# Unpacking 4-bit weights of the last layer during an earlier attention instead of during the attention just before it

## The chip, the core and the metric

The kernel runs on one core of a Trainium2 chip. A core has a matrix engine (TensorE, PE in the rows; PEld is its weight load), three engines for elementwise work (VectorE = DVE, ScalarE = ACT, GpSimd = POOL) and SyncE (SP), which here only issues DMA transfers. Each engine works through its own list of instructions in order; the lists are tied together by semaphores alone. The metric is the device time of one execution in microseconds (us).

## What is computed

The state x has 8 batches of 128 rows by 512 (float32). Four layers run over it; each is an attention over `ctx_4096` and a feed-forward part, both added to x:

```python
x = x + _L2_xattn_ref(_layernorm(x), ctx_4096, mask, Wq, Wk, Wv, Wo, ...)   # wide attention: 32 heads of 128
x = x + _L2_ffn_ref(_layernorm(x), weight)                                   # product of values rounded to fp8
x = x + _L3_xattn_ref(_layernorm(x), ctx_4096, ctx_4096)                     # lag attention: FFT, top lags, softmax
x = x + _L3_ffn_ref(_layernorm(x), w1, s1, w2, s2, w3, s3)                   # silu(x W1) * (x W3), then W2
```

W1, W3 (1376 x 512) and W2 (512 x 1376) come packed. Each 32-bit word holds one byte with two signed 4-bit values, `w >> 4` and the sign-extended low four bits; each group of 64 values has one float32 scale:

```python
msb = w >> 4
lsb = (w & 15 ^ 8) - 8
deq = concatenate([msb, lsb], 1).reshape(-1, 64) * s[:, None]
```

## The kernel before

The layers before L2 are not touched. From there on four stages follow each other, each ended by `end_stage`, a barrier that all engines meet: `wide_attention`, `quantised_ffn`, `lag_attention`, `streamed_packed_ffn`.

**wide_attention** runs over steps s: 8 groups of 4 heads times 8 batches are 64 steps, with some ten steps of weight preparation ahead of step 0 and five behind step 63. In a step PE makes the scores of batch s, the queries of s + 4, a quarter of the next group's keys or values, the mix of s - 3 and the output projection of s - 4; each engine has its fixed list of such parts. Matmuls are done in three passes on float16 halves (`pair_matmul`, lines 67 to 69). DVE's list of a step begins with `low_of_heads` (tile a_o_lo), `maxima` (a_masked, a_negmax: the softmax's mask and maximum, which wait for the step's scores) and `add_to_x` (x_state); `add_to_x` frees the one bank into which PE puts the next output projection. SP turns queries, keys and probabilities by DMA (DMA_TRANSPOSE) and loads the next group's weights.

**quantised_ffn** loads, on SP, the tables of the lag attention (`spectra.load`), and then all packed words that the next two stages need first: W2's words and scales (`load_down`), and the first 128 rows of W1 and W3 (`load_first`, "the first tile"). SP waits for them at the stage's end.

**lag_attention** takes batches through a pipeline of steps i = 0 to 10 (`over_steps`): DVE multiplies the query spectra by the key spectra (tile x_q_prod), PE turns them into correlations, DVE finds the nine largest of each row (MAX8 and MATCH_REPLACE8 on x_nine, x_left), PE and DVE form the output. `AHEAD` splits the layer norm that opens the stage into batches 0, 1 and the rest. W2 is prepared here by `DownWeight` in 11 chunks of 512 values:

- `unpack` (DVE): two tensor_scalar shifts of 128x256 int32 into `ints`;
- `to_half` (ACT): to float16, over the place of the words; `UNPACK` says when: chunks 0 to 2 and 3 to 6 ahead of the first step, 7 and 8 in step 0, 9 and 10 in step 1;
- `scale` (POOL): times the scales; `high` (ACT) and `low` (POOL): split into two float16 halves; SP turns a quarter of W2 whenever its chunks are ready.

At the stage's end the layer norm of the last part begins: ACT normalises batches 0 to 3 (`rows_ahead`), DVE takes their low halves (`low_of_row`), SP turns them (`turn_row`). Between these stand the same five operations for the first tiles of W1 and W3; SP's last two issues of the stage, `turn_first`, wait for POOL's `low` of them.

**streamed_packed_ffn** begins with PE's product of batches 0 to 3 and the first tile of W1 (`first_in`, `xt_in` are what it waits for). The other tiles of W1 and W3 are unpacked while it runs.

Of the kernel before, what the change touches and what calls it, by code (L numbers as in the profile page):

```python
# [8 lines left out]
P = 128  # L9
B = 8  # L10
DIM = 512
KT = DIM // P
EPS = 1e-5
WS = 64.0
# [1376 lines left out]
def wide_attention(K, A, wq, wk, wv, wo, mask=None, qw=None, kw=None, quant=None, nxt=None):  # L1391
# [12 lines left out]
    with ExitStack() as c:  # L1404
# [131 lines left out]
        with nc.Block() as block:  # L1536
            @block.sync
            def _(sp):
# [22 lines left out]
                for s in steps:  # L1561
# [149 lines left out]
            def _(act):  # L1711
# [68 lines left out]
                for s in steps:  # L1780
# [10 lines left out]
                    for u in live(s):  # L1791
                        exponentials(u)

            @block.vector
            def _(dve):
# [92 lines left out]
                for s in steps:  # L1888
# [30 lines left out]
            def _(pool):  # L1919
# [723 lines left out]
def quantised_ffn(K, Q, spectra, packed):  # L2643
# [8 lines left out]
    with ExitStack() as c:  # L2652
# [7 lines left out]
        largest_done, chain, words_here = (K.sem(f"f2_{n}") for n in ("largest", "chain", "words"))  # L2660
# [193 lines left out]
def lag_attention(K, S, packed):  # L2854
# [9 lines left out]
    with ExitStack() as c:  # L2864
# [18 lines left out]
        UNPACK = {-2: (0, 1, 2), -1: (3, 4, 5, 6), 0: (7, 8), 1: (9, 10)}  # L2883
        ROWS = packed.FIRST_ROWS
        W1, W3 = down.FIRST["w1"], down.FIRST["w3"]
# [19 lines left out]
        with nc.Block() as block:  # L2905
            @block.sync
            def _(sp):
                packed.load_scales(sp)
                for i in range(B + 2):
# [76 lines left out]
            def _(act):  # L2986
# [64 lines left out]
                for i in (-2, -1):  # L3051
                    for chunk in UNPACK[i]:
                        down.to_half(act, chunk)
# [3 lines left out]
            def _(dve):  # L3057
# [10 lines left out]
                def step(f, m, l, n, j, i):  # L3068
# [6 lines left out]
                    for chunk in UNPACK.get(i, ()):  # L3075
                        down.unpack(dve, chunk)
# [759 lines left out]
```

## Time and profile before

| | |
|---|---|
| median of 3 runs | 1548.2 us (1547.27 to 1550.75) |
| the profiled execution's own time | 1544.96 us |
| its span, first to last instruction | 1543.2 us |
| mean granted clock of TensorE | 0.964 of full speed |
| busy: PE, DVE, ACT, POOL | 90%, 69%, 49%, 46% of the span |

The span is what the trace shows in detail; 1.8 us of the profiled execution lie around it. Its time is 3.2 us below the median of the runs, so sums made in the trace are carried to the median as differences.

### The profile page before, as it was taken

What the parts mean: (1) busy time and instruction counts of PE and PEld (TensorE: products, weight loads), DVE (VectorE), ACT (ScalarE), POOL (GpSimd) and SP (SyncE); (2) the same over time, 40 slices, a digit from 0 to 9 for tenths busy, and PEclk for the clock granted to TensorE, in tenths of its full rate; (3) what the DMA queues carried; (4) which work ended last, traced back from release to release, by engine and by line L of the source; (5) the groups of instructions that cost most, each with busy time, mean ns of one, the idle gap of its engine ahead of it and who ended that gap; (6) DMA issues with size and microseconds to landing.
All of it is one profiled execution on the core that took longest, in us unless ns stands there. A gap on an engine that the chain in (4) does not pass through costs nothing. (4 is left out here: it accounts for less than half of the span.)

```text
span 1543.2 us, 31400 instructions
## 1 busy us (share of the span) xinstructions
PE 1385.5 (90%) x11336; PEld 829.9 (54%) x11352; DVE 1068.9 (69%) x2142; ACT 752.6 (49%) x2417; POOL 717.0 (46%) x736
## 2 busy tenths in 40 slices
PE   5898599997999999659999999999998677879998
PEld 4776244445777777326555555555554234434444
DVE  7997565636667766558878878788778789956212
ACT  4677363223434433237666666666654356555111
POOL 4887451002434435726666666666555115744000
PEclk9999799999999999989999999999999789989999
DMA  7999572216999988556666566544434402456000
GB/s 184 187 172 175 128 167 39 41 28 147 176 183 188 164 147 144 96 133 153 122 132 114 117 129 122 107 112 108 103 73 83 145 3 41 102 89 111 16 18 28
DMA packets 524138, 174.63 MB, mean 113 GB/s; under 512 B 482528, under 2 KB 507424, under 8 KB 523856
## 3 DMA queue, kind: packets, MB, share of 16 engines
q1 hardware_dynamic: 523984, 172.62, 57.9%
q8 instruction: 92, 1.51, 0.4%
q14 instruction: 62, 0.51, 0.1%
HBM read 53.27 MB, written 2.10 MB: 36 GB/s over the span
## 5 line engine op out<-in xcount | busy, mean ns | idle before, releaser
L1929 POOL TENSOR_TENSOR a_q_ss<-a_q_ss,half 128x4 f32<-128x4 f32 x64 | 89.3, 1395 | 183.5 <-DVE a_k_ss L1845 93.0
L67 PE MATMUL bank<-a_wq_hi,xn_pair 128*128 128x512 f16 (+1 forms) x384 | 139.8, 364 | 20.3 <-DVE a_wq_lo L1880 16.9
L1764 ACT ACTIVATE a_probs<-a_masked,a_negmax 128x128 f32<-128x128 f32 x256 | 99.6, 390 | 95.6 <-DVE a_negmax L1816 95.6
L1286 POOL TENSOR_TENSOR a_p_hl<-a_probs,a_p_hl 128x512 f16<-128x512 f32 x64 | 74.3, 1161 | 142.5 <-DVE a_p_hl L1210 142.5
L68 PE MATMUL bank<-a_wq_lo,xn_pair 128*128 128x512 f16 (+1 forms) x384 | 139.7, 364 | 0.0
L69 PE MATMUL bank<-a_wq_hi,xn_pair 128*128 128x512 f16 (+1 forms) x384 | 139.6, 364 | 0.0
L67 PE MATMUL bank<-a_wo_hi,a_o_hi 128*128 128x512 f16 x256 | 98.0, 383 | 9.9 <-DVE x_state L1832 9.9
L69 PE MATMUL bank<-a_wo_hi,a_o_lo 128*128 128x512 f16 x256 | 98.0, 383 | 0.0
L68 PE MATMUL bank<-a_wo_lo,a_o_hi 128*128 128x512 f16 x256 | 98.0, 383 | 0.0
L1813 DVE TENSOR_TENSOR a_masked<-bank,a_mask 128x512 f32<-128x512 f32 x64 | 44.1, 690 | 70.2 <-PE bank L69 70.1
L1944 POOL TENSOR_TENSOR a_normal<-a_probs,a_recip 128x512 f32<-128x512 f32 x64 | 89.7, 1401 | 5.0
L716 POOL TENSOR_TENSOR a_p_hl<-a_probs,a_p_hl 128x512 f16<-128x512 f32 x64 | 78.3, 1234 | 25.4 <-DVE a_p_hl L627 15.1
L67 PE MATMUL bank<-a_k_t,a_q_t 128*128 128x128 f16 (+1 forms) x384 | 81.1, 237 | 0.4 <-DMA a_q_t<-a_q_hl 0.4
L69 PE MATMUL bank<-a_k_t,a_q_t 128*128 128x128 f16 (+1 forms) x384 | 81.0, 237 | 0.0
L68 PE MATMUL bank<-a_k_t,a_q_t 128*128 128x128 f16 (+1 forms) x384 | 81.0, 237 | 0.0
L489 ACT ACTIVATE a_probs<-bank,a_negmax 128x128 f32<-128x128 f32 x256 | 72.3, 380 | 17.6 <-DVE a_negmax L620 17.3
L1775 ACT ACTIVATE a_o_hi<-bank 128x512 f16<-128x512 f32 x64 | 38.1, 596 | 86.3 <-PE bank L69 86.2
L1203 DVE TENSOR_REDUCE a_negmax<-bank 128x2 f32<-128x512 f32 x64 | 42.8, 690 | 50.3 <-PE bank L69 50.3
L3666 DVE SCALAR_TENSOR_TENSOR f_h<-bank,f_h 128x512 f32<-128x512 f32 (+1 forms) x22 | 15.2, 689 | 85.6 <-PE bank L69 76.0
L1130 ACT ACTIVATE a_probs<-bank,a_negmax 128x256 f32<-128x256 f32 x128 | 53.3, 472 | 32.5 <-DVE a_negmax L1203 32.5
L1732 ACT ACTIVATE a_qn<-bank 128x128 f32<-128x128 f32 x256 | 67.1, 288 | 3.1 <-PE bank L69 3.1
L1937 POOL TENSOR_TENSOR a_recip<-a_total,minus_one 128x4 f32<-128x4 f32 x64 | 64.8, 1012 | 6.9 <-ACT a_probs L1764 6.9
(459 smaller groups left out, 4983.0 us busy)
## 6 DMA issues: line engine op xcount, KB each, us to landing
a_no<-in_L_xattn_Wo SPq DMA_DIRECT2D x9, 1024.0 KB, 5.9
a_nq<-in_L_xattn_Wq SPq DMA_DIRECT2D x8, 1024.0 KB, 5.8
a_n_wq<-in_L_xattn_Wq SPq DMA_DIRECT2D x4, 768.0 KB, 5.8
a_n_wo<-in_L_xattn_Wo SPq DMA_DIRECT2D x4, 768.0 KB, 5.4
a_nk<-in_L_xattn_Wk SPq DMA_DIRECT2D x9, 256.0 KB, 3.0
a_nv<-in_L_xattn_Wv SPq DMA_DIRECT2D x9, 256.0 KB, 4.0
f_v_hat<-in_L_ffn_w SPq DMA_DIRECT2D x2, 1152.0 KB, 5.9
x_state<-in_x SPq DMA_DIRECT2D x8, 256.0 KB, 4.2
```

Source lines behind the costliest of these rows:

```text
L67: pe.matmul(out, lh, rh, start=start, stop=False)
L68: pe.matmul(out, lh, rl, start=False, stop=False)
L69: return pe.matmul(out, ll, rh, start=False, stop=stop)
L489: m = act.activation(probs[t % PS][:, h * P:(h + 1) * P], s_bank[t][:, h * P:(h + 1) * P], ACT.Exp, bias=negmax[t % 4][:, h:h + 1])
L716: pool.tensor_tensor(p_hl[t % PS][:, 1, :], probs[t % PS][:, :], p_hl[t % PS][:, 0, :], ALU.subtract).then_inc(plo_done.sem, 1)
L1130: m = act.activation(probs[u % PROBS][:, n, :], s_bank[(s, t)][:, n * KTL * P:(n + 1) * KTL * P], ACT.Exp, bias=negmax[u % 4][:, n:n + 1])
L1286: pool.tensor_tensor(p_hl[s % PN][:, 1, t, :], probs[unit(s, t) % PROBS][:, :, :].rearrange("p h n -> p (h n)"), p_hl[s % PN][:, 0, t, :], ...
L1732: m = act.activation(dst[:, h, :], src[:, h, :], ACT.Square, scale=1.0 / WS, accum_out=sums[:, h:h + 1])
L1764: m = act.activation(probs[s % 2][:, h, :], src, ACT.Exp, bias=negmax[s % 2][:, h:h + 1], accum_out=total[s % 2][:, h:h + 1])
L1929: pool.tensor_tensor(r[:, :], r[:, :], K.half[:, 0:n], ALU.pow).then_inc(root_done.sem, 1)
L1937: pool.tensor_tensor(recip[s % 2][:, :], total[s % 2][:, :], K.minus_one[:, :], ALU.pow).then_inc(recip_done.sem, 1)
L1944: m = pool.tensor_tensor(normal[s % 2][:, t, :, :], probs[s % 2][:, :, t * P:(t + 1) * P], by, ALU.mult)
```

## The change

`PackedFirst` is new. It holds the packed words, their scales and the first tiles in memory of its own from the wide attention on, loads them there, and does three things in the wide attention's steps: `unpack` on DVE, `halves` on ACT and `scale_first` on POOL, each called as the last or nearly last part of its engine's step. Thirteen pieces (first tile of W1, of W3, then W2's 11 chunks) take their turn every fourth step from step 3 on. Piece n has its two shifts on DVE at steps 3 + 4n and 5 + 4n and its copy to float16 on ACT at 6 + 4n; the two first tiles are also scaled on POOL at 8 + 4n, split on ACT at 9 + 4n and on DVE at 10 + 4n. The rows of `xn_rows`, unused until the wide attention's end, serve as `ints` and `flat`. In the lag attention `unpack` and `to_half` are gone, `scale`, `high` and `low` of W2's chunks stay, and nothing of the first tiles is left but `turn_first`, which SP now issues in step 7.

```diff
@@ wide_attention: SP, ACT, DVE, POOL, at the end of a step
+                    down.load(sp, s)
...
+                    down.halves(act, s)
...
+                    down.unpack(dve, s)
                     if 0 <= s - ROWS - 1 < quant.ahead:
                         row_ahead(s - ROWS - 1)
...
+                    down.scale_first(pool, s)
@@ quantised_ffn, SP
                 spectra.load(sp)
-                packed.load_down(sp, words_here)
-                packed.load_first(sp, words_here)
-                sp.wait_ge(words_here, 96)
@@ lag_attention, SP
+                    if i == B - 1:
+                        sp.wait_ge(qb_bank.filled("x"), qb_bank.n_filled("x", B - 1))
+                        for m in ("w1", "w3"):
+                            packed.turn_first(sp, m)
...
-                for m in ("w1", "w3"):
-                    sp.wait_ge(down.lo_done.sem, down.lo_done.count(down.FIRST[m]))
-                    packed.turn_first(sp, m)
@@ lag_attention, ACT and DVE (in a step, at the stage's end, and ahead of the steps)
-                    for chunk in UNPACK.get(i, ()):
-                        down.to_half(act, chunk)
...
                         rows_ahead(0)
-                        down.to_half(act, W1)
                         rows_ahead(2)
-                        down.to_half(act, W3)
-                        down.high(act, W1)
-                        down.high(act, W3)
...
-                for chunk in UNPACK[-1]:
-                    down.unpack(dve, chunk)
                 over_steps(step)
@@ lag_attention, POOL
                 over_steps(step)
-                down.scale(pool, W1)
-                down.scale(pool, W3)
-                down.low(pool, W1)
-                down.low(pool, W3)
@@ new: PackedFirst
+    WORD_PARTS = [(0, 3), (3, 6), (6, 9), (9, 11)]
+    BEGIN = 3
...
+    def load(self, sp, s):
+        if s == 0:
+            for m in self.FIRST:
+                w, scale = self.source[m]
+                sp.dma_start(self.first_words[m][:, :], w.rearrange("(o j) c -> o (j c)", j=self.PER)[0:P, :]).then_inc(self.first_here, 16)
+                sp.dma_start(self.first_scales[m][:, :], scale.rearrange("(o j) -> o j", j=2 * self.PER)[0:P, :]).then_inc(self.first_here, 16)
+            sp.dma_start(self.scales[:, :], self.source["w2"][1].rearrange("(p n) -> p n", p=P)).then_inc(self.scales_here, 16)
+        if s in (2, 4, 6, 8):
...
+    def piece_at(self, s, late, every):
+        i, odd = divmod(s - self.BEGIN - late, every)
+        return [self.pieces[i]] if odd == 0 and 0 <= i < len(self.pieces) else []
+
+    def unpack(self, dve, s):
+        for part in range(2):
+            for n in self.piece_at(s, 2 * part, 4):
...
+                if part == 0:
...
+                    dve.tensor_scalar(dst[:, 0:g, 0, :], src, 4, None, ALU.arith_shift_right)
+                else:
+                    dve.tensor_scalar(dst[:, 0:g, 1, :], src, 28, 28, ALU.logical_shift_left,
+                                      ALU.arith_shift_right).then_inc(self.ints_done.sem, 1)
...
+    def halves(self, act, s):
+        for n in self.piece_at(s, 3, 4):
+            i = self.pieces.index(n)
+            act.wait_ge(self.ints_done.sem, self.ints_done.count(n))
+            act.activation(self.values(n), self.ints[i % 2][:, 0:self.groups(n), :, :].rearrange("p j h c -> p (j h c)"),
+                           ACT.Copy, scale=WS).then_inc(self.half_done.sem, 1)
```

How the change moves instructions is shown at three places. First DVE in the wide attention, from the end of step 7 into step 8, in the changed kernel (a2 is this attention; in the rows of the trace its tiles begin with a_):

```order
L1882 SCALAR_TENSOR_TENSOR a2_wo1_lo<-a2_no,a2_wo1_hi 128x512
L1882 SCALAR_TENSOR_TENSOR a2_wq0_lo<-a2_nq,a2_wq0_hi 128x4x128
L3274 TENSOR_SCALAR xn_rows<-down_first_words_w3 128x4x64
L1828 TENSOR_TENSOR a2_o0_lo<-bank6,a2_o0_hi 128x512
L1815 TENSOR_TENSOR a2_masked0<-bank4,a2_mask 128x512
L1818 TENSOR_REDUCE a2_negmax0<-a2_masked0 128x4
L1834 SCALAR_TENSOR_TENSOR x_state<-bank7,x_state 128x512
```

The shift (line 3274) is new between the weights' low halves and the next step's first part; the other rows stood there before, two line numbers lower. Second DVE at the opening of the lag attention (x3), before:

```order
L3155 TENSOR_SCALAR xn_rows<-x_state,x3_mv,x3_rstd 128x512 x2
L99 BN_STATS stats<-x_state 128x6 x6
L3065 BN_AGGR x3_mv<-stats 128x2 x6
L3369 TENSOR_SCALAR down_ints1<-down_words 128x4x64
L3370 TENSOR_SCALAR down_ints1<-down_words 128x4x64
...
L3074 TENSOR_TENSOR x3_q_prod0<-bank0,x3_k_hat 128x512
L3074 TENSOR_TENSOR x3_q_prod0<-bank1,x3_k_hat 128x512
...
L3369 TENSOR_SCALAR down_ints0<-down_words 128x3x64
L3370 TENSOR_SCALAR down_ints0<-down_words 128x3x64
L3080 MEMSET x3_spacer 128x1
L3082 MAX x3_nine<-x3_corr0 128x8 x4
```

and in the changed kernel:

```order
L3140 TENSOR_SCALAR xn_rows<-x_state,x3_mv,x3_rstd 128x512 x2
L99 BN_STATS stats<-x_state 128x6 x6
L3056 BN_AGGR x3_mv<-stats 128x2 x6
L3065 TENSOR_TENSOR x3_q_prod0<-bank0,x3_k_hat 128x512
L3065 TENSOR_TENSOR x3_q_prod0<-bank1,x3_k_hat 128x512
L3065 TENSOR_TENSOR x3_q_prod1<-bank0,x3_k_hat 128x512
L3065 TENSOR_TENSOR x3_q_prod1<-bank1,x3_k_hat 128x512
L3069 MEMSET x3_spacer 128x1
L3071 MAX x3_nine<-x3_corr0 128x8 x4
```

All 22 shifts of W2's chunks have left this list: eight stood between the layer norm and the first product, four between the first step's products and the second's, four between these and the first maximum. Third SP at the end of the lag attention, before:

```order
L3355 DMA_TRANSPOSE f3_w2_t<-ctx_lo 128x11x128 x2
L3274 DMA_TRANSPOSE xn_pair<-xn_rows 128x8x128 x4
L3278 DMA_TRANSPOSE xn_rows<-f3_first_halves_w1 128x8x128
L3278 DMA_TRANSPOSE xn_rows<-f3_first_halves_w3 128x8x128
L2905 UNCONDITIONAL_BRANCH
```

and in the changed kernel:

```order
L3355 DMA_TRANSPOSE xn_rows<-down_first_halves_w1 128x8x128
L3355 DMA_TRANSPOSE xn_rows<-down_first_halves_w3 128x8x128
L3404 DMA_TRANSPOSE f3_w2_t<-ctx_hi 128x11x128 x2
L3342 DMA f3_v_hat<-in_L3_ffn_w3 128x9x256
L3343 DMA f3_v_hat<-in_L3_ffn_w3 96x256
L3404 DMA_TRANSPOSE f3_w2_t<-ctx_lo 128x11x128 x2
L3351 DMA_TRANSPOSE xn_pair<-xn_rows 128x8x128 x4
L2904 UNCONDITIONAL_BRANCH
```

The two turns of the first tiles have moved from the list's end to ahead of the third quarter of W2; the list now ends with the four rows of x.

## Rows read from the trace of the kernel before

**Rows 1.** Busy time per engine (instructions), granted clock, DMA share, GB/s, by stretch.

```profile
820.00:860.00 40.00, 40.00 (x320) 23.64 (x319) 32.21 (x61) 24.77 (x110) 25.52 (x25) 1.00 0.69 135
...
1257.00:1364.00 107.00, 71.75 (x260) 40.23 (x260) 92.65 (x303) 59.15 (x146) 60.42 (x64) 0.88 0.33 67
...
1400.00:1440.00 40.00, 40.00 (x187) 18.19 (x186) 19.69 (x38) 16.92 (x30) 11.67 (x11) 1.00 0.52 86
```

**Rows 2.** Timeline of DVE, wide attention, steps 7 to 9: start, duration.

```profile
759.09 1.53 DVE L1880 SCALAR_TENSOR_TENSOR a_wq_lo<-a_nq,a_wq_hi 128x512 f16<-128x512 f32 x1
760.54 0.68 DVE L1826 TENSOR_TENSOR a_o_lo<-bank,a_o_hi 128x512 f16<-128x512 f32 x1
761.14 0.68 DVE L1813 TENSOR_TENSOR a_masked<-bank,a_mask 128x512 f32<-128x512 f32 x1
...
762.45 0.68 DVE L1832 SCALAR_TENSOR_TENSOR x_state<-bank,x_state 128x512 f32<-128x512 f32 x1
...
768.87 0.69 DVE L1813 TENSOR_TENSOR a_masked<-bank,a_mask 128x512 f32<-128x512 f32 x1 [1.71 <-PE bank L69]
```

**Rows 3.** Timeline of PE, step 8: the first matmul of the output projection.

```profile
765.34 0.38 PE L67 MATMUL bank<-a_wo_hi,a_o_hi 128*128 128x512 f16 x1
```

**Rows 4.** Line by line: duration ns least/median/most, first and last start.

```profile
L3369 DVE TENSOR_SCALAR down_ints<-down_words x11: 259/294/927, 1259.1 to 1277.3; 128x256 int32<-128x256 int32 x10, 128x192 int32<-128x192 int32 x1
L3370 DVE TENSOR_SCALAR down_ints<-down_words x11: 280/286/1248, 1259.3 to 1277.6; 128x256 int32<-128x256 int32 x10, 128x192 int32<-128x192 int32 x1
L3394 ACT ACTIVATE down_words<-down_ints x11: 507/629/631, 1259.6 to 1278.0; 128x512 f16<-128x512 int32 x10, 128x384 f16<-128x384 int32 x1
L3405 POOL TENSOR_TENSOR down_flat<-f_first_words_w,f_first_scales_w x2: 1042/1042/1042, 1354.2 to 1357.4; 128x512 f32<-128x512 f16 x2
L3093 DVE TENSOR_TENSOR x_beyond<-x_nine x8: 197/630/896, 1280.6 to 1339.2; 128x36 f32<-128x36 f32 x8
```

**Rows 5.** SP's waits, 690 to 760 us: total, times, longest.

```profile
SPq L1568 <- DVE a_k_nat L1863: 25.9, 5, 11.0
```

**Rows 6.** SP's waits, 1214 to 1260 us: total, times, longest.

```profile
SPq L2668 <- PEq L2668: 30.5, 1, 30.5
```

**Rows 7.** Timeline of all engines, lag attention, opening to the first maximum.

```profile
1261.34 3.78 PE L2939 MATMUL bank<-xn_rows,x_spec 128*128 128x512 f32 x4 [5.63 <-DVE xn_rows L3155]
...
1265.77 0.26 DVE L3369 TENSOR_SCALAR down_ints<-down_words 128x256 int32<-128x256 int32 x1
...
1267.86 1.28 DVE L3074 TENSOR_TENSOR x_q_prod<-bank,x_k_hat 128x512 f32<-128x512 f32 x2
...
1269.24 3.75 PE L2955 MATMUL bank<-x_inv,x_q_prod 128*128 128x128 f32 x16 [4.12 <-DVE x_q_prod L3074]
...
1275.84 0.38 DVE L3369 TENSOR_SCALAR down_ints<-down_words 128x256 int32<-128x256 int32 x1
1276.02 2.02 PE L2955 MATMUL bank<-x_inv,x_q_prod 128*128 128x128 f32 x16 [0.83 <-issue]
...
1277.84 0.28 DVE L3082 MAX8 x_nine<-x_corr 128x8 f32<-128x128 f32 x1
```

**Rows 8.** Timeline of all engines, end of the lag attention into the last stage.

```profile
1353.50 0.61 ACT L3394 ACTIVATE f_first_words_w<-down_ints 128x512 f16<-128x512 int32 x1
1354.02 0.80 ACT L2999 ACTIVATE xn_rows<-x_state,f_shift,f_rstd 128x512 f32<-128x512 f32 x1
...
1356.23 2.63 SPq L3274 DMA_TRANSPOSE xn_pair<-xn_rows  x2
...
1358.27 0.69 DVE L3141 TENSOR_TENSOR x_state<-bank,x_state 128x512 f32<-128x512 f32 x1
...
1359.62 2.61 SPq L3278 DMA_TRANSPOSE xn_rows<-f_first_halves_w  x2
1363.79 0.29 DVE L3638 TENSOR_SCALAR f_v_hat<-f_v_hat 128x256 int32<-128x256 int32 x1 [4.83 <-PEq L104]
...
1365.40 0.59 PE L67 MATMUL bank<-xn_pair,xn_rows 128*128 128x512 f16 x1 [10.78 <-PEq L3539]
```

More of the change, by code:

```diff
@@ L3150, in _ @@
                 take_stats(0)
-                for chunk in UNPACK[-2]:
-                    down.unpack(dve, chunk)
                 dve.wait_ge(eps_done.sem, eps_done.count("pow", 0))
@@ new lines, in __init__ @@
+        self.first_words = {m: keep(f"first_words_{m}", [P, self.PER * self.GROUP], I32) for m in self.FIRST}
+        self.first_scales = {m: keep(f"first_scales_{m}", [P, 2 * self.PER], F32) for m in self.FIRST}
+        self.first_halves = {m: keep(f"first_halves_{m}", [P, 2, DIM], F16) for m in self.FIRST}
+        self.ints = [K.xn_rows[:, i, :].bitcast(I32).rearrange("p (j h c) -> p j h c", j=self.PER, h=2) for i in range(2)]
+        self.flat = [K.xn_rows[:, 2 + i, :] for i in range(2)]
@@ new lines, in __init__ @@
+        self.first = {n: m for m, n in self.FIRST.items()}
+        self.chunks = list(range(-(-self.HID * self.PER // self.CHUNK)))
+        self.pieces = list(self.first) + self.chunks
+        step = lambda n, of: Steps(K.sem(f"early_{n}"), of)
+        self.ints_done, self.half_done = step("ints", self.pieces), step("half", self.pieces)
+        self.scaled_done, self.hi_done, self.lo_done = (step(n, list(self.first)) for n in ("scaled", "hi", "lo"))
+        self.first_here, self.scales_here = K.sem("down_first_here"), K.sem("down_scales_here")
@@ new lines, in __init__, with groups, words_of, scales_of @@
+        self.words_here = [K.sem(f"down_words_here{i}") for i in range(len(self.WORD_PARTS))]
+    def groups(self, n):
+        return self.PER if n in self.first else min(self.PER, self.W2G - self.PER * n)
+    def words_of(self, n):
+        if n in self.first:
+            return self.first_words[self.first[n]][:, :]
+        at = self.CHUNK // 2 * n
+        return self.words[:, at:at + self.groups(n) * self.GROUP]
+    def scales_of(self, n):
+        at = 2 * self.PER * n
+        return self.scales[:, at:at + 2 * self.groups(n)]
@@ new lines, in halves @@
+    def halves(self, act, s):
[4 more added lines that the diff above has]
+                           ACT.Copy, scale=WS).then_inc(self.half_done.sem, 1)
+        for n in self.piece_at(s, 6, 4):
+            if n in self.first:
+                act.wait_ge(self.scaled_done.sem, self.scaled_done.count(n))
+                act.activation(self.first_halves[self.first[n]][:, 0, :], self.flat[self.pieces.index(n)],
+                               ACT.Copy).then_inc(self.hi_done.sem, 1)
@@ new lines, in scale_first @@
+    def scale_first(self, pool, s):
+        for n in self.piece_at(s, 5, 4):
+            if n in self.first:
+                by = self.first_scales[self.first[n]][:, :].unsqueeze(2).to_broadcast([P, 2 * self.PER, self.GROUP])
+                pool.wait_ge(self.half_done.sem, self.half_done.count(n))
+                pool.tensor_tensor(self.flat[self.pieces.index(n)].rearrange("p (j c) -> p j c", c=self.GROUP),
+                                   self.values(n).rearrange("p (j c) -> p j c", c=self.GROUP), by, ALU.mult).then_inc(self.scaled_done.sem, 1)
@@ L3315, in __init__ @@
         self.rows = rows[0:W.PER]
-        step = lambda n: Steps(K.sem(f"down_{n}"), self.pieces)
-        self.ints_done, self.half_done, self.scaled_done, self.hi_done, self.lo_done = (
-            step(n) for n in ("ints", "half", "scaled", "hi", "lo"))
+        step = lambda n: Steps(K.sem(f"down_{n}"), self.chunks)
+        self.scaled_done, self.hi_done, self.lo_done = (step(n) for n in ("scaled", "hi", "lo"))
         self.blank, self.turned = K.sem("down_blank"), W.turned
@@ L3323, in at, with flat_row @@
         return [n for n in self.chunks if self.when[n] + later == i]
-    def groups(self, n):
-        return self.W.PER if n in self.first else min(self.W.PER, self.W.W2G - self.W.PER * n)
-    def flat_row(self, tiles, n):
-        return tiles[n % 2][:, 0:self.groups(n), :, :].rearrange("p j h c -> p (j h c)")
+    def flat_row(self, n):
+        return self.flat[n % 2][:, 0:self.early.groups(n), :, :].rearrange("p j h c -> p (j h c)")
     def parts(self, n):
-        if n in self.first:
-            halves = self.W.first_halves[self.first[n]]
-            yield halves[:, 0, :], halves[:, 1, :], self.flat_row(self.flat, n)
-            return
         first, last, W = self.CHUNK * n, min(self.CHUNK * n + self.CHUNK, self.W.HID * self.W.PER), self.W
```

111 lines of the change are left out of this document (43 added, 68 removed).

## The prediction

> **What bounds the kernel now.** I read the busy times by stretch first, to see which engine sets the pace of each stage that the change touches [rows 1]. In the middle of the wide attention PE is busy for all 40.00 of 40 us at full granted clock, while DVE works 32.21, ACT 24.77 and POOL 25.52 us: the step time is PE's. In the lag attention it is the other way round: DVE is busy 92.65 of 107 us, PE 71.75. In the last stage PE is again busy 40.00 of 40. So operations on DVE, ACT or POOL are cheap in the first, dear in the second, and the last stage only passes on the moment at which its PE may begin. Then I read the timelines. In the wide attention I looked for the step with the least room [rows 2]: DVE ends step 7 late with a weight's low half (1.53 us), goes on without a pause through a_o_lo and a_masked, and adds to x_state at 762.45. PE's next output projection, which needs that bank back, begins at 765.34 [rows 3]. In step 9 DVE waits for PE's scores again (1.71 us idle ahead of a_masked) and has caught up. In the lag attention I looked for unpacking that DVE does while something downstream waits [rows 7], and at the end of that stage for the operation that ends last [rows 8].
>
> **The change, part by part.**
>
> *Added to the wide attention.* 26 shifts on DVE, 13 copies on ACT, two scalings on POOL, two high and two low halves. A shift alone took 0.26 to 0.29 us, and up to 0.93 or 1.25 where POOL was at work beside it; a copy 0.63, a scaling 1.04 [rows 4]. ACT has 15 us and POOL 14 us of idle time in 40 us [rows 1]; one copy in four steps lies in that. For DVE the place decides. A first shift falls at the end of steps 3, 7, 11 and so on. After step 7 DVE has no idle time, so the shift pushes everything in step 8 back by its full length: x_state would end at 762.45 + 0.68 = 763.13 plus at most 1.25, that is 764.38, and PE wants the bank at 765.34. The room is 765.34 - 763.13 = 2.21 us, larger than the longest shift seen; 1.71 us of idle time in step 9 then take the delay back. The second shift, two steps later, meets idle time of its own. I take 0. Bounds: 0, and 26 x 1.25 = 32.5 us if every shift stood on PE's path.
>
> On 26 shifts that will often meet POOL the Trainium skill has a rule that speaks against the change. The rows show shifts of 0.28 and of 1.25 us for the same work [rows 4], and the low half of 1.53 us beside others of 0.68 [rows 2]. The page SBUF — State Buffer, section "Who interferes with whom", says that DVE in a mode that uses two ports, which tensor_scalar can enter, and GpSimd take one pair of ports in turns, and that the loser "fully blocks". By that rule the long shifts are waits for one POOL operation; the trace agrees. By the rule a shift would cost at most a POOL operation plus itself, still less than the room, and the sum stays as it is.
>
> *DMA and SP.* Nine issues are new in the wide attention (five in step 0, one each in steps 2, 4, 6, 8). The longest kind of issue in these rows took 2.61 / 2 = 1.3 us [rows 8], so nine cost SP at most 11.7 us. Queued behind them are the turns of queries, keys and probabilities, for which PE waits some steps later. The cover is SP's own waiting: 25.9 us for key rows alone between 690 and 760 us [rows 5]. Price 0; if step 0's five issues delayed everything once, up to 6.5 us, no more than a step of the steady pace (768.87 - 761.14 = 7.7 [rows 2]), and the turns run more than a step ahead of their use. In the quantised part six issues go away; SP then waited 30.5 us for the other engines [rows 6], so this gains 0.
>
> *Removed ahead of the lag attention's steps.* Chunks 0 to 2 stand where DVE would otherwise wait for POOL's root: 0 (at most some tenths). Chunks 3 to 6 do stand in the way. The first shift began at 1265.77, the first product x_q_prod at 1267.86 [rows 7]. What that product needs from PE was there at 1261.34 + 3.78 = 1265.12. Without the shifts it starts at 1265.77: **2.09 us** gained, and PE, which had idled 4.12 us for it, follows.
>
> *Removed in steps 0 and 1.* Chunks 7 and 8 lie under PE's correlations, where DVE waits anyway: 0. Chunks 9 and 10 began at 1275.84 and the first maximum at 1277.84 [rows 7]; its input, PE's correlations, ended at 1269.24 + 3.75 = 1272.99 and needs a short copy. **2.00 us** gained. From there to the end of the pipeline DVE has hardly a pause, so both gains reach the stage's end.
>
> *Given back.* With the maximum earlier, POOL's chunk work, whose start doesn't move as far, falls on x_beyond of the first step. That operation takes 0.20 us alone and up to 0.90 beside POOL [rows 4]. 0 to 0.70 us; I take the median less the least, 0.63 - 0.20, so **0.4 us** lost.
>
> *The stage's end.* SP's last issues, the turns of the first tiles, begin at 1359.62 and end at 1359.62 + 2.61 = 1362.23; DVE starts the last stage at 1363.79, PE at 1365.40 [rows 8]. In the changed kernel SP ends with the turn of x's row 3, now over at 1356.23 + 2.63 = 1358.86. That itself comes earlier, since ACT's copy for W1 stood ahead of rows 2 and 3: 1354.02 - 1353.50 = 0.52 us. So SP is done at 1358.34, **3.89 us** sooner. What is late next is DVE's last addition, 1358.27 + 0.69 - 0.52 = 1358.44, which ties with it. In their new place the two turns wait for the last query spectrum, which PE makes in step 6; SP's next transfer is due in step 8, so nothing is held.
>
> *Sum.* 2.09 + 2.00 - 0.40 + 3.89 = 7.6 us. In the profiled execution's own time 1544.96 - 7.6 = 1537.4; the runs' median is 3.2 us higher, 1548.2 - 7.6 = **1540.6 us**. In its own terms, the lag attention's steps should begin and end about 3.7 us sooner and the last stage's PE 7.6 us sooner.
>
> **The rivals.**
>
> A. *Only one of the two places pays.* Either the barrier is held by something else at the end (DVE, or the last stage's PE by the landing of x's row 3, issued last now), or DVE's early gain is lost again in a wait for PE or POOL. For it: the tie at 1358.44 above, and PE stood for only part of the opening. Against it: PE waited 10.78 us for the last stage, and DVE had idled 4.83 there [rows 8]. Left is 2.09 + 2.00 - 0.40 = 3.7 or 3.9 us: about 1544.4.
>
> B. *The clock adds to it.* PE's first 16 correlation matmuls took 3.75 us, the next 16 took 2.02 [rows 7]: the first, after 4.12 us of idling, ran at or near the lower of its two levels (1.2 GHz), the second near 2.4 GHz, and the granted clock of the whole stretch is 0.88 [rows 1]. With half the pause the level could rise sooner: up to 3.75 - 2.02 = 1.7 us more, and without the loss of 0.4 a gain of 9.7 us, 1538.5.
>
> C. *Nothing to see.* The removed shifts were only the visible part of a wait that another engine would have ended just as late; 0 to 3 us remain, about 1547. Against it: PE's part for both moved operations had ended 2.7 us and more before they started.
>
> D. *Slower.* In the wide attention a shift waits behind POOL for longer than the rows of the lag attention show, x_state frees PE's bank too late, and PE loses what exceeds 2.21 us, 26 times. It decides from 2.21 + (7.6 + 3.1) / 26 = 2.6 us for a shift on. At 3 us: 26 x 0.79 = 20.5 us lost, 1548.2 - 7.6 + 20.5 = 1561. For it: POOL works 25.5 of 40 us there [rows 1]. Against it: the longest shift took half of that, and the second shifts meet idle time. The page's rule above works for this rival, with one POOL operation as its limit.
>
> **How the numbers follow.** Forecast (a gain of about 5 to 9 us) 0.70; A 0.11; B 0.07; C 0.06; D 0.06. The predicted time is the forecast's, 1540.6. The range takes in A and B: from 1538.5, less 0.9 us by which the lowest of the runs lies under their median, to 1544.4 plus 1.1 for a somewhat smaller A; 1537.6 to 1545.5. C and D stay outside. A measurement of this kernel can tell about 0.2%, 3.1 us, from no change. Faster by more: forecast, B and nearly all of A, 0.86; within it: C and the rest of A, 0.08; slower: D, 0.06.
>
> **What would show it.** Right: in the wide attention PE still busy 40.00 of 40 us and steps of about 7.7 us; x_q_prod following the layer norm at once; the first maximum some 4 us nearer to the stage's start; at the end SP's four turns of x as the last issues, and some 6.9 us rather than 10.8 of PE idling at the last stage's start. Wrong: PE idle ahead of the output projection on x_state, once every four steps (D); DVE idle ahead of the first maximum or of the second step's products (A, C); a barrier that comes no sooner after SP's last issue (A).

## The result

The changed kernel took 1539.25 us (median of 4 runs, 1536.3 to 1540.15) beside 1549.47 us of the kernel before (4 runs, 1547.27 to 1551.68): a ratio of 0.9937, 95% interval 0.9921 to 0.9954. In a second comparison it was 1540.76 beside 1548.48 us, 0.9957 (0.9943 to 0.9970). So it is 0.4 to 0.6% faster, 7.7 and 10.2 us by the medians; 1540.6 was predicted.

The two profiled executions differ by less, 1543.2 and 1538.4 us of span. The missing part lies ahead of the change: step 0 of the wide attention begins at 709.97 us in the profile of before and at 712.99 in that of the changed kernel, though nothing in front of it differs. The stretches must therefore be measured from their own starts. This table does that, with a second profile of each kernel beside the first (from the experiments below):

| us | before | before, 2nd | changed | changed, 2nd |
|---|---|---|---|---|
| step 0 of the wide attention (first a_masked) | 709.97 | 714.94 | 712.99 | 713.68 |
| from there to the lag attention's first operation | 547.53 | 547.08 | 547.60 | 547.44 |
| from there: first product x_q_prod | 10.36 | 10.36 | 7.94 | 7.95 |
| first maximum | 20.34 | 21.35 | 15.39 | 15.43 |
| first operation behind x_beyond of that step | 23.24 | 24.25 | 19.20 | 19.24 |
| last maximum | 79.14 | 80.06 | 75.22 | 75.29 |
| ACT's row 0 of the last layer norm | 93.27 | 94.15 | 88.75 | 88.82 |
| end of SP's last issue | 104.73 | 105.62 | 96.40 | 96.48 |
| PE's first matmul of the last stage | 107.90 | 108.74 | 99.55 | 99.58 |
| from there to the end | 177.80 | 177.74 | 178.26 | 178.30 |

The second row also holds the nine new transfers of the wide attention and the six that left the quantised part: neither shows in it. The lag attention and the barrier behind it are 8.35 us shorter (9.16 in the second pair). The span's 4.8 us are 8.35 - 3.02 (the later step 0) - 0.07 - 0.46 (the last stage).

### The profile page after: what moved, and what is told of

Same layout as the page of the kernel before. It is cut to its first block and busy times, and to the rows that moved or that the text cites. A ratio compares the mean times of both kernels' runs of the same rounds, so it can differ in the third digit from the quotient of the medians.

```text
span 1538.4 us, 31418 instructions
## 1 busy us (share of the span) xinstructions
PE 1389.7 (90%) x11352; PEld 829.4 (54%) x11352; DVE 1087.4 (71%) x2144; ACT 751.6 (49%) x2417; POOL 713.7 (46%) x734
```

## The profile after

The busy times by stretch, to be held against [rows 1] (us; then busy time and instructions of PE, PEld, DVE, ACT and POOL, granted clock, DMA share, GB/s):

```profile
820.00:860.00 40.00, 40.00 (x320) 23.61 (x319) 35.02 (x64) 25.31 (x113) 24.78 (x23) 1.00 0.63 124
1260.00:1360.00 100.00, 69.77 (x260) 39.64 (x260) 84.93 (x280) 51.66 (x133) 54.83 (x61) 0.91 0.34 72
1400.00:1440.00 40.00, 40.00 (x187) 18.71 (x186) 15.67 (x30) 13.58 (x24) 8.94 (x8) 1.00 0.35 66
```

DVE works 2.8 us more per 40 us of the wide attention, and PE is still busy 40.00 of 40. The same step as in [rows 2] and [rows 3], step 7 into 8, in the timeline of all engines:

```profile
762.14 1.53 DVE L1882 SCALAR_TENSOR_TENSOR a_wq_lo<-a_nq,a_wq_hi 128x512 f16<-128x512 f32 x1
763.59 0.69 DVE L3274 TENSOR_SCALAR xn_rows<-down_first_words_w 128x256 int32<-128x256 int32 x1
764.20 0.68 DVE L1828 TENSOR_TENSOR a_o_lo<-bank,a_o_hi 128x512 f16<-128x512 f32 x1
...
766.12 0.68 DVE L1834 SCALAR_TENSOR_TENSOR x_state<-bank,x_state 128x512 f32<-128x512 f32 x1
...
768.39 0.38 PE L67 MATMUL bank<-a_wo_hi,a_o_hi 128*128 128x512 f16 x1
```

The shift pushes x_state back, which ends at 766.80; PE takes the bank at 768.39, so 1.59 us of the 2.21 are left. Up to step 59 the least room was 1.35 us (step 16). In the last steps, from 60 on, PE waits for x_state in both kernels, six times, and follows it by 0.15 us; the last shift comes before that, in step 53. The steps together took 475.70 us, against 475.66 before.

The opening of the lag attention, in the timeline of all engines, against [rows 7]:

```profile
1260.59 0.11 DVE L3135 MEMSET x_nine<- 128x64 f32 x1 [0.98 <-PEq L104]
...
1264.11 3.78 PE L2939 MATMUL bank<-xn_rows,x_spec 128*128 128x512 f32 x4 [5.29 <-DVE xn_rows L3140]
1268.11 0.51 DVE L3056 BATCH_NORM_AGGREGATE x_mv<-stats 128x2 f32<-128x6 f32 x6
1268.53 1.26 DVE L3065 TENSOR_TENSOR x_q_prod<-bank,x_k_hat 128x512 f32<-128x512 f32 x2
1269.89 3.72 PE L2955 MATMUL bank<-x_inv,x_q_prod 128*128 128x128 f32 x16 [2.00 <-DVE x_q_prod L3065]
1273.44 1.88 PE L2939 MATMUL bank<-xn_rows,x_spec 128*128 128x512 f32 x4
1274.51 0.69 DVE L3065 TENSOR_TENSOR x_q_prod<-bank,x_k_hat 128x512 f32<-128x512 f32 x1 [4.71 <-PE bank L2939]
1275.98 0.29 DVE L3071 MAX8 x_nine<-x_corr 128x8 f32<-128x128 f32 x1
1277.77 2.04 POOL L3419 TENSOR_TENSOR down_flat<-down_words,down_scales 128x512 f32<-128x512 f16 x2
1278.78 1.08 DVE L3082 TENSOR_TENSOR x_beyond<-x_nine 128x36 f32<-128x36 f32 x1
```

The product follows the layer norm at once, and the maximum follows the second product. The last row is the price: x_beyond takes 1.08 us, and before it took 0.20:

```profile
1280.63 0.20 DVE L3093 TENSOR_TENSOR x_beyond<-x_nine 128x36 f32<-128x36 f32 x1
```

And the end of the stage, against [rows 8]:

```profile
1351.62 5.37 SPq L3351 DMA_TRANSPOSE xn_pair<-xn_rows  x4
1356.33 0.69 DVE L3128 TENSOR_TENSOR x_state<-bank,x_state 128x512 f32<-128x512 f32 x1
1358.53 0.29 DVE L3652 TENSOR_SCALAR f_v_hat<-f_v_hat 128x256 int32<-128x256 int32 x1 [1.50 <-PEq L104]
1360.14 0.58 PE L67 MATMUL bank<-xn_pair,xn_rows 128*128 128x512 f16 x1 [6.94 <-PEq L3553]
```

SP's last issues are the four turns of x, done at 1356.99; DVE's last addition ends at 1357.02, the tie that was foreseen. PE idles 6.94 us ahead of the last stage instead of 10.78.

## The experiments

Each of the first four puts one part of the change back. Their times differ from the changed kernel's by no more than two such ratios can differ by chance, so the traces decide; times in them are again from the lag attention's first operation.

**1. The turns of the first tiles at the end again.**

```diff
-                    if i == B - 1:
-                        sp.wait_ge(qb_bank.filled("x"), qb_bank.n_filled("x", B - 1))
-                        for m in ("w1", "w3"):
-                            packed.turn_first(sp, m)
...
                     packed.turn_row(K, sp, b)
+                for m in ("w1", "w3"):
+                    packed.turn_first(sp, m)
```

> The changed kernel with one thing put back: SP turns the two first tiles as its last two issues of the lag attention, behind the four rows of x. The halves have long been there, so the two turns cost only themselves, 2.61 us for two in the rows of before. If SP's last issue holds the barrier (my theory), the last stage's PE begins 2.6 us later from the start of the lag attention than in the changed kernel (102.2 instead of 99.55 us) and the time rises by 2.6 us, about 0.17%. If the barrier is held by something else as well (rival A: DVE's last addition, which ends within 0.1 us of SP in the changed kernel), it stays under 0.5 us. If the turns do not add up behind the rows of x but overlap with them, it is between, 1.3 us.

It took 1542.06 us, ratio to before 0.9951 (0.9936 to 0.9965). Its timeline at the stage's end:

```profile
1352.29 5.36 SPq L3349 DMA_TRANSPOSE xn_pair<-xn_rows  x4
1356.99 0.69 DVE L3126 TENSOR_TENSOR x_state<-bank,x_state 128x512 f32<-128x512 f32 x1
1357.69 2.72 SPq L3353 DMA_TRANSPOSE xn_rows<-down_first_halves_w  x2
1361.94 0.29 DVE L3650 TENSOR_SCALAR f_v_hat<-f_v_hat 128x256 int32<-128x256 int32 x1 [4.26 <-PEq L104]
1363.52 0.59 PE L67 MATMUL bank<-xn_pair,xn_rows 128*128 128x512 f16 x1 [9.66 <-PEq L3551]
```

DVE's addition is over at 1357.68, but DVE starts the next stage only 1.53 us behind SP's last turn (1360.41), as it did 1.54 us behind it in the changed kernel. From ACT's row 0 to SP's end it is 10.41 us, against 7.65 in the changed kernel: 2.76 us. SP holds the barrier; the half of rival A that says something else does is out. Nor does the landing of x's row 3 hold PE: its first matmul comes 1.6 us behind DVE's first operation of the stage in before, in the changed kernel and here, where that row had landed 3.8 us before the matmul. From the stage's start PE is only 1.73 us later, 101.28, because in this execution x_beyond of the first step took 0.20 us; experiment 6 says why that can be.

**2. Chunks 3 to 6 ahead of the first product again.** `DownWeight` gets back `ints`, `unpack` and `to_half`, for these chunks alone; the wide attention leaves them out.

```diff
+        UNPACK = {-1: (3, 4, 5, 6)}
...
                 take_stats(1)
+                for chunk in UNPACK.get(-1, ()):
+                    down.unpack(dve, chunk)
                 over_steps(step)
```

> The changed kernel with W2's chunks 3 to 6 unpacked again between the layer norm of the lag attention and its first product (8 shifts on DVE, 4 copies on ACT); all else stays early. Theory: the first product starts 2.1 us later from the stage's start (10.0 instead of 7.94 us), everything behind it keeps the delay, and the whole time rises by 2.1 us; if the clock of PE matters there too, by 2.6. Rival: the delay is swallowed by DVE's wait of 4.71 us for PE's second pair of spectra (the last maxima come no later than 75.0 us from the stage's start), and the time stays within 0.5 us. A third case, that it is the chunks' POOL and ACT work and not DVE's place in the row that counted, would give no delay of the product either.

It took 1542.59 us, ratio 0.9955 (0.9941 to 0.9969). The timeline of DVE and PE, in which the stage starts at 1263.81:

```profile
1271.76 0.26 DVE L3436 TENSOR_SCALAR down_ints<-down_words 128x256 int32<-128x256 int32 x1
...
1273.85 1.28 DVE L3071 TENSOR_TENSOR x_q_prod<-bank,x_k_hat 128x512 f32<-128x512 f32 x2
1275.23 3.75 PE L2956 MATMUL bank<-x_inv,x_q_prod 128*128 128x128 f32 x16 [4.11 <-DVE x_q_prod L3071]
1278.78 2.57 PE L2940 MATMUL bank<-xn_rows,x_spec 128*128 128x512 f32 x4
...
1282.00 0.29 DVE L3079 MAX8 x_nine<-x_corr 128x8 f32<-128x128 f32 x1
```

The product comes at 10.04 us, 2.10 later than in the changed kernel, and the delay stays: last maximum at 77.28 (2.06 later), PE's first matmul at 101.62 (2.07 later). DVE's wait of 4.71 us for the second spectra swallows nothing, since PE makes these behind the correlations that wait for the first product. PE's idling of 4.11 instead of 2.00 us is back as well, and with it slower spectra (2.57 instead of 1.88 us): the first maximum is 2.80 us later, not 2.10. This first step's x_beyond, at 0.44, gives that back.

**3. Chunks 9 and 10 ahead of the first maximum again** (`UNPACK = {1: (9, 10)}`, in the same way).

> The changed kernel with W2's chunks 9 and 10 unpacked again ahead of the first maximum (4 shifts on DVE, 2 copies on ACT); all else stays early. Theory: the first maximum starts 2.0 us later (17.4 instead of 15.4 us from the stage's start), but x_beyond of that step then falls behind POOL's two scalings and goes back from 1.08 to about 0.20 us, so that from there on the delay is 1.1 us, and the time rises by 1.1 us. Rival 1: x_beyond stays long, and the time rises by 2.0 us. Rival 2: DVE had slack for both, and the time stays within 0.3 us.

It took 1542.09 us, ratio 0.9956 (0.9942 to 0.9971). The timeline:

```profile
1275.47 0.83 DVE L3436 TENSOR_SCALAR down_ints<-down_words 128x256 int32<-128x256 int32 x1
1276.22 1.25 DVE L3437 TENSOR_SCALAR down_ints<-down_words 128x256 int32<-128x256 int32 x1
...
1277.92 0.28 DVE L3079 MAX8 x_nine<-x_corr 128x8 f32<-128x128 f32 x1
1280.71 0.20 DVE L3090 TENSOR_TENSOR x_beyond<-x_nine 128x36 f32<-128x36 f32 x1
...
1285.27 3.62 PE L2956 MATMUL bank<-x_inv,x_q_prod 128*128 128x128 f32 x16
...
1289.68 0.19 DVE L3102 TENSOR_REDUCE x_total<-x_nine_e 128x4 f32<-128x36 f32 x1 [0.80 <-ACT x_nine_e L3030]
```

The four shifts took 2.45 us here (1275.47 to 1277.92), and the maximum comes 2.53 us later. x_beyond is short again, as the theory says: behind it the delay is 1.63 us. But at the last maximum it is 2.60. The missing 0.97 us went in the second step: PE's correlations took 3.62 us there (granted 0.50), ACT's copy of them stood ahead of x_nine_e, and DVE waited 0.80 us for that (0.34 in the changed kernel) and 0.37 for PE right behind it. In the changed kernel these correlations were nearly as slow (3.47 us, granted 0.54), but DVE, held up by x_beyond, came later and waited less; in experiment 2, at 1.95 us, x_beyond's gain was kept. So 1.1 us was too low and rival 1's 2.0 too; the part is worth 1.6 us of DVE time, and a further us where PE's clock is low in the second step.

**4. Chunks 0 to 2, 7 and 8 back** (`UNPACK = {-2: (0, 1, 2), 0: (7, 8)}`).

> The changed kernel with the five chunks put back that I costed at nothing: W2's chunks 0 to 2 while DVE waits for POOL's root, and 7 and 8 under PE's first correlations (10 shifts on DVE, 5 copies on ACT). Theory: the layer norm comes 0.3 us later, because POOL's first step beside the shifts took 0.53 instead of 0.23 us, and the rest is hidden: 0.3 us in all, not to be told from none in the time. Rival: they are on the path as much as the others are (10 shifts of 0.28 us, two of them stretched to 1 us beside POOL), and the time rises by 2 us or more.

It took 1539.30 us, ratio 0.9937 (0.9923 to 0.9950). The first product comes at 8.27 us, 0.33 later, because POOL's first operation beside the shifts took 0.53 instead of 0.23 us. At the first maximum the delay is still 0.29 us (15.68). At x_beyond, which takes 0.46 us here instead of 1.08, it turns into a lead, and PE's last stage starts at 99.14, 0.41 sooner than in the changed kernel. So these chunks cost 0.3 us up to the first maximum and the rest of them is hidden, as the prediction had it ("at most some tenths"); the shorter wait for POOL gave back more than that here.

**5. More shifts in the wide attention.** Each of the 26 shifts is preceded by one, three or fifteen more of the same shape, into rows that nothing reads.

```diff
+                    for _ in range(3):
+                        self.again(dve, src, g)
                     dve.tensor_scalar(dst[:, 0:g, 0, :], src, 4, None, ALU.arith_shift_right)
```

One more:

> The changed kernel with every shift of the wide attention followed on DVE by one more of the same shape (128x256 words into unused rows; 26 more). In the changed kernel x_state ends 2.30 us ahead of the first matmul of the output projection in a step that a shift does not delay, and 1.35 to 2.05 us ahead in steps 8, 16, 24, 32, 40 and 48. Theory (the room is what counts): another shift of 0.69 to 1.13 us still fits, so 64 steps take 475.7 us as before, the room in those six steps falls to some 0.2 to 1.4 us, and the time stays within 1 us. Rival (each shift costs because DVE waits for POOL again, or because something other than x_state is late): from 26 x 0.3 = 8 us on.

Three more:

> The changed kernel with every shift of the wide attention followed on DVE by three more of the same shape (78 more). Theory: three more of 0.69 to 1.13 us are 2.1 to 3.4 us, more than the 1.35 to 2.05 us of room in steps 8, 16, 24, 32, 40 and 48; PE then waits for x_state in these steps, 0.5 to 2 us each, and elsewhere the idle time of DVE (1.1 to 1.7 us a step) and 2.30 us of room still take nearly all of it: 3 to 15 us slower in all. Rival 1 (the room is larger than x_state's, since the added delay is taken back in every step): 0. Rival 2 (the room was used up, each added shift costs itself): 78 x 0.7 = 55 us and more.

Fifteen more:

> The changed kernel with every shift of the wide attention followed on DVE by fifteen more (390 more). With three more the 64 steps took 476.0 us, since shifts behind the first one cost only 0.21 us each (a wait for POOL falls on a group once), and x_state kept 0.15 us of room in steps 8 and 16, 0.73 in steps 24 to 48, 1.3 to 1.6 after a second shift. Twelve more of 0.21 us are 2.5 us a place. Theory (x_state's room is the cover, and it is finite): 2 x 2.5 + 5 x 1.8 + 19 x 1.0 to 1.2, so 20 to 35 us slower than the changed kernel, with PE idle ahead of the output projection. Rival (DVE's idle time in a step, not x_state, is the cover, 5 us of it in 7.8): under 8 us.

One more: 1538.83 us, ratio 0.9938 (0.9916 to 0.9960), the 64 steps 475.66 us; the least room up to step 59 fell from 1.35 to 1.16 us. Three more: 1539.21 us, 0.9946 (0.9925 to 0.9966), 476.02 us. My theory for three more was wrong: 78 added shifts cost 0.3 us. Step 7 into 8 in that kernel's timeline:

```profile
767.44 1.09 DVE L3295 TENSOR_SCALAR xn_rows<-down_first_words_w 128x256 int32<-128x256 int32 x3
768.46 0.28 DVE L3279 TENSOR_SCALAR xn_rows<-down_first_words_w 128x256 int32<-128x256 int32 x1
...
770.57 0.68 DVE L1834 SCALAR_TENSOR_TENSOR x_state<-bank,x_state 128x512 f32<-128x512 f32 x1
...
771.40 0.38 PE L67 MATMUL bank<-a_wo_hi,a_o_hi 128*128 128x512 f16 x1
```

Four shifts take 1.22 us together, not four times 0.69: one wait for POOL, then about 0.2 us each. In the 440 us from 740 on DVE is busy 395.35 us instead of 375.28, 0.26 us for each added shift. x_state ends 0.15 us ahead of PE, so here, and once more in step 16, the room is used up: 0.15 us is the distance that PE also keeps in the last steps, where it waits for x_state, and so it is no room. The 2.21 us of the prediction were 2.06 to be used.

Fifteen more: 1591.15 us, 1.0284 (1.0264 to 1.0303), 52.0 us more than in the changed kernel from step 0 to the lag attention, above my 20 to 35. PE's waits there, from 740 us on (total us, times, longest):

```profile
PE bank L67 <- DVE x_state L1834: 34.0, 31, 4.0
PE bank L67 <- DVE a_o_lo L1828: 14.6, 11, 2.3
```

In the changed kernel these are 10.0 and 1.2 us. The cover is x_state's room, and it is finite; beyond it the delay reaches a_o_lo as well, which I had left out. PE's granted clock falls to 0.98 over the steps (1.00 in the changed kernel), and the same 4015 matmuls are busy for 11.8 us longer. With the waits' 24.0 and 13.4 us more that is 49 of the 52.0. The rival, under 8 us, is out; its idle time of DVE was misstated, since that is 5 us in 40, not in one step.

**6. POOL's second scaling one step later** (`WHEN = [0, 0, 1, 2, 2, 3, 4, 5, 6, 7, 7]`, was `[0, 0, 1, 1, 2, ...]`).

> The changed kernel with POOL scaling W2's chunk 3 one step later (step 2 instead of 1), so that in step 1 it has one scaling, not two, behind the low halves. Theory (x_beyond of the first step waits for POOL's second scaling): that x_beyond goes from 1.08 back to about 0.2 us, the second one gets longer instead, from 0.20 to up to 1 us, and the last maxima move by less than 0.5 us. Rival: x_beyond is long for another reason and stays at 1.08.

One execution took 1539.68 us. The scalings of POOL and x_beyond in its timeline:

```profile
1277.10 1.05 POOL L3419 TENSOR_TENSOR down_flat<-down_words,down_scales 128x512 f32<-128x512 f16 x1
1278.18 0.20 DVE L3082 TENSOR_TENSOR x_beyond<-x_nine 128x36 f32<-128x36 f32 x1
1284.38 0.20 DVE L3082 TENSOR_TENSOR x_beyond<-x_nine 128x36 f32<-128x36 f32 x1
1284.42 2.06 POOL L3419 TENSOR_TENSOR down_flat<-down_words,down_scales 128x512 f32<-128x512 f16 x2
```

The first x_beyond is back at 0.20 us: it was the second scaling that it waited for. In the changed kernel that scaling began at 1278.77 and took 1.04 us, x_beyond was ready at 1278.78 and ended at 1279.86, 0.05 us behind it. Here the second step's x_beyond starts 0.04 us ahead of a scaling and takes 0.20. So the rest of my theory missed: the second x_beyond did not get longer (the third went from 0.90 to 1.02), and the last maxima came 0.78 us sooner, not within 0.5. A few hundredths decide about 0.9 us, but not by chance alone: of six profiles whose opening is the changed kernel's, five have the long x_beyond (1.02 to 1.09 us), in four of them with the scaling's start within 0.01 us of its own. The sixth is experiment 1, where POOL's chunk work lay 0.93 us earlier and x_beyond missed it; PE's first correlations had taken 2.79 instead of 3.72 us there. The gain does not reach the last stage (99.80 us), because eight of PE's matmuls near the stage's end took 6.9 instead of 4.0 us in this execution.

The Trainium skill, page SBUF — State Buffer, section "Who interferes with whom", names two things here: that a DVE instruction with two inputs in SBUF contends with a GpSimd instruction that reads SBUF, and that "Issue order, not op shape, decides who blocks." The traces agree with both: wherever x_beyond took longer than 0.20 us, it ended 0.05 us behind an operation of POOL that had begun before it or within 0.01 us of it, and where POOL's began 0.04 us behind it, it took 0.20.

**7. Without x_beyond.** If DVE paces the stage, the cure for its wait is to have ACT make the exponentials of the nine largest.

```diff
-                        dve.tensor_tensor(beyond[:, :, :], nine[:, :, 0:9], nine[:, :, 0:1].broadcast_to([P, KT, 9]),
-                                          ALU.subtract).then_inc(own.sem, 1)
...
-                        act.wait_ge(own.sem, own.count("beyond", m))
-                        act.activation(nine_e[:, :, :], beyond[:, :, :], ACT.Exp).then_inc(nine_done.sem, 1)
+                        act.wait_ge(own.sem, own.count("next8", m))
+                        for k in range(KT):
+                            r = act.activation(nine_e[:, k, :], nine[:, k, 0:9], ACT.Exp, bias=negmax[:, k:k + 1])
+                        r.then_inc(nine_done.sem, 1)
```

> The changed kernel without x_beyond: ACT makes the exponentials of the nine largest itself, as four operations with the negated maximum as bias, in place of one on x_beyond. DVE loses 8 operations that took 5.6 us in the changed kernel (0.20 us alone, up to 1.08 beside POOL). Theory (DVE paces the lag attention to its end, and the wait for POOL in x_beyond is lost time): the last maxima come some 5 us sooner from the stage's start (70.0 instead of 75.0 us) and the time falls by about 5 us. Rival 1: ACT's four operations come too late for the sum behind them, and half of it or more is lost in a new wait on ACT: 0 to 2.5 us. Rival 2: the wait for POOL moves on to another DVE operation that reads two operands, and only the 1.6 us of eight unhindered ones are won.

It took 1533.76 us, ratio 0.9913 (0.9892 to 0.9933). To set it beside the changed kernel, both were timed on one chip, and the kernel before was profiled again:

> The version without x_beyond once more, on the same chip as the changed kernel. Theory: it beats the changed kernel by 4 us (4.1 us between the first and the last maximum in its first profile), 0.25%. Rival: the 4 us of that profile are lost elsewhere in the timed runs, and the two are within 2 us.

> The changed kernel once more, to be timed on the same chip as the version without x_beyond. Theory: 0.5 to 0.65% faster than before (8 to 10 us), 8.4 us of it in the lag attention and at its end, as in the first profile (7.4 to 9.3 us by whether x_beyond of the first step falls behind POOL's second scaling, which a tie decides). Rival: the first comparison was favourable, and it is 0.3% or less.

> The kernel before, once more, for a second profile. Its first profile reached step 0 of the wide attention at 709.97 us, the eight profiles of other versions at 711.2 to 716.1, though nothing ahead of that step differs. If this is the scatter of the stages in front (my theory), the second profile of before comes within 711 to 716 us there. If the change itself delays the stages in front of it (rival), it stays at 710. In the tail of the lag attention, PE's 8 matmuls ahead of the last rows took 5.6 us in before and 4.0 us in the changed kernel, worth 0.60 us: if that belongs to the kernel before, the stretch from the last maximum to ACT's first row is 14.1 us again, if to the phase of PE's clock in one execution, anything between 13.5 and 14.6.

There it took 1535.14 us, 0.9913 (0.9899 to 0.9927), and the changed kernel 1540.76, 0.9957 (0.9943 to 0.9970): 5.6 us, and intervals that do not meet. It beats both kernels. The changed kernel's 0.43% is a little less than the 0.5 to 0.65 that I expected of it. The first and the last maximum without x_beyond:

```profile
1277.60 0.29 DVE L3073 MAX8 x_nine<-x_corr 128x8 f32<-128x128 f32 x1
...
1333.37 0.66 DVE L3073 MAX8 x_nine<-x_corr 128x8 f32<-128x128 f32 x3
```

That is 55.8 us instead of 59.9, 4.1 of the 5 us that I expected, and PE's last stage starts at 94.87 us instead of 99.58. ACT's four operations cost more than its one did (7.0 instead of 1.9 us in all, in the lag attention), which nothing waits for but once, 0.5 us.

Most of this wait is older than the change: the eight x_beyond took 4.64 us in the kernel before and 5.58 in the changed one. The cure was not tried on the kernel before.

The second profile of before reaches step 0 at 714.94 us, among the others: the 709.97 of the first was scatter, and with it the small difference of the two spans.

## Why the prediction was right, step by step

The terms, from the first pair of profiles:

| step | predicted us | measured us |
|---|---|---|
| 26 shifts, 13 copies and the rest in the wide attention | 0 | 0.07 |
| chunks 3 to 6 | 2.09 | 2.10 (experiment 2) |
| chunks 0 to 2 | 0, at most some tenths | 0.32 at the first product (0.33 in experiment 4) |
| chunks 9 and 10 | 2.00 | 2.00, and 0.53 of PE's clock |
| x_beyond beside POOL | -0.40 | -0.91 |
| stage's end, SP | 3.89 | 3.81 |
| PE's clock at the end of the pipeline | none | 0.60 |
| rest | 0 | -0.10 |
| sum behind the wide attention | 7.6 | 8.35 |

In the second pair the sum is 9.16: chunks 9 and 10 stood for 2.60 us there, because two of their shifts waited for POOL (1.09 and 1.13 us), and the spectra behind the first correlations for 0.91. The terms that the prediction named worked as it said, but that the sum came so near is in part luck: 1.45 us that it did not hold (0.53 and 0.60 of PE's clock, 0.32 of chunks 0 to 2) stand against 0.51 too little for x_beyond and 0.18 elsewhere.

**The cover in the wide attention** held for the reason given, x_state's room in front of PE, and experiment 5 shows it used up and exceeded. The step read for it, with 2.21 us, was not the tightest one: step 30 had 1.93 us, and in the steps from 60 on, behind the last shift, PE waited. The longest shift, 1.13 us, would have fitted in step 30 too. The shifts there met POOL nearly always (duration least/median/most in ns, first and last start):

```profile
L3274 DVE TENSOR_SCALAR xn_rows<-down_words x11: 347/694/1131, 793.5 to 1107.0; 128x256 int32<-128x256 int32 x10, 128x192 int32<-128x192 int32 x1
L3276 DVE TENSOR_SCALAR xn_rows<-down_words x11: 344/1131/1132, 809.2 to 1122.7; 128x256 int32<-128x256 int32 x10, 128x192 int32<-128x192 int32 x1
```

The longest is 1.13 us, inside the bound of 1.25 and far from rival D's 2.6.

**The opening.** Both removed groups stood in the way as read, and both gains reached the end: rival C is out. **The mis-sized term** is the one given back: x_beyond lost 0.88 us, not 0.4. I had taken the median of the rows less the least; the wait here was for an operation of POOL that had just begun, so for its whole 1.04 us. The upper bound of 0.70 did not hold it.

**The stage's end** is the best-shown term: 3.81 in the profile, 2.76 of it the two turns (experiment 1), the rest, not tested by itself, would be ACT's copy and the turns' lateness.

Rival A is out too, since both places paid. **Rival B** had the mechanism and the wrong place. The first 16 correlations still took 3.72 us, nearly all at the lower level (granted 0.53). What sped up were the spectra behind them (1.88 instead of 2.41 us; 0.99 instead of 0.79), worth 0.53, and the matmuls ahead of the last rows of x. The granted clock (third column from the right) over the spectra, before and in the changed kernel:

```profile
1272.80:1275.30 2.50, 2.39 (x5) 0.81 (x4) 0.76 (x2) 2.27 (x4) 0.38 (x1) 0.79 0.00 0
```
```profile
1273.40:1275.40 2.00, 1.93 (x6) 0.62 (x4) 0.73 (x2) 1.75 (x4) 0.00 (x0) 0.99 0.00 0
```

The shorter pause goes with this in every profile: correlations and spectra together took 5.95 to 6.37 us where PE had idled 4.1 to 4.4 us (both of before, experiment 2), and 5.2 to 5.5 us in the eleven others, where it had idled 2.0 to 2.3. The granted clock ahead of the last rows, in the second profile of before, then of the changed kernel:

```profile
1349.50:1355.60 6.10, 5.47 (x8) 1.80 (x8) 6.07 (x13) 0.58 (x1) 5.37 (x7) 0.72 0.46 86
```
```profile
1343.90:1349.60 5.70, 3.97 (x8) 1.35 (x8) 5.11 (x11) 0.67 (x2) 5.19 (x7) 1.00 0.48 89
```

Eight matmuls took 5.47 us at a mean of 0.72 and 3.97 at 1.00, worth 0.60 us at ACT's row 0. From the last maximum to that row it was 14.1 us in both profiles of before and 13.5 in both of the changed kernel and in six of its variants, but 14.6 in experiment 6 and 14.2 with fifteen more shifts, which have the change too. PE's pauses ahead of these matmuls were alike in both kernels (1.2, 0.4, 1.5 and 0.7 us). Whether the change keeps the level up there, or shifts the phase of it by luck, stays open.

**Also open**: the last stage takes 177.1 to 178.4 us over all profiles, and the changed kernel's two lie at the upper end. Its length goes with PE's granted clock in its first 10 us: 0.85 in the shortest, 0.80 in both profiles of before, 0.73 in both of the changed kernel, 0.72 in the longest. What sets how soon the clock rises there was not tried.

## What to carry to other kernels

Ask of added work which transfer of a buffer it delays and how long before its use that transfer is done: here nearly every step had some 2 us to spare at one addition, and that number, not DVE's 80% of busy time, said that 26 operations would cost nothing and where more would. In the stage that an engine paces, take work off that engine where something behind it waits; the same work in its existing waits costs next to nothing (chunks 0 to 2, 7 and 8). Look for the two-operand operation of DVE that falls behind a POOL operation, above all when DVE has got ahead of its neighbours, and move that to another engine: it was worth 5.6 us here, more than half of the change itself.

## What the runs showed of the hardware

- A wait for POOL falls on a run of DVE shifts nearly once, not on each: alone in their place they took 0.69 and 1.13 us, three more brought 0.26 us each.
- A POOL operation that began within 0.01 us of x_beyond cost it 0.9 us, one that began 0.04 us behind it nothing; variants of one kernel showed 0.20, 0.44, 0.46 and 1.08 us for the same x_beyond.
- The start of a stage scattered by 6 us between executions (step 0 at 709.97 to 716.07 us in 14 profiles), while its own length kept within 0.9 us but for fifteen more shifts. A difference of a few us is read from the stretch that the change touches.
